# Second-layer block loads issued by SyncE, and another order of transposes, products, sets and FFN copies

## What is computed

```python
xn = layernorm(x)
h = relu(xn @ Wself0 + mean_of_neighbours(xn) @ Wneigh0 + b0)
gnn = h @ Wself1 + mean_of_neighbours(h) @ Wneigh1 + b1
q, k = relu(xn @ Wq + bq), relu(xn @ Wk + bk)        # 16 heads of 64
v = xn @ Wv + bv
mix = ((q @ k.T) / (1250 * 64) @ v) @ Wo + bo         # head by head
x = x + gnn + mix
y = layernorm(x)
out = x + quant(gelu(quant(y) @ ternary(w1).T)) @ ternary(w2).T
```

## Time and profile before

| | |
|---|---|
| median of 3 runs | 1304.35 us |
| the profiled execution | 1304.18 us |
| its span | 1302.4 us |
| TensorE busy | 1290.4 us, 99% |
| VectorE busy | 845.7 us, 65% |
| ScalarE busy | 652.0 us, 50% |
| GpSimd busy | 93.9 us, 7% |
| granted TensorE clock | 1.00 |

### The profile page before, as it was taken

One profiled execution on the slowest core, in us unless ns is written; L12 is line 12 of the kernel. 1 busy time (PEld: TensorE's weight loads), 2 busy tenths in 40 slices (PEclk: granted clock), 3 DMA queues, 4 the chain that ended last, 5 costly groups with the idle time before them and its releaser, 6 DMA issues.

```text
span 1302.4 us, 18781 instructions
## 1 busy us (share of the span) xinstructions
PE 1290.4 (99%) x6370; PEld 613.4 (47%) x6370; DVE 845.7 (65%) x1472; ACT 652.0 (50%) x895; POOL 93.9 (7%) x91
## 2 busy tenths in 40 slices
PE   9999999999999999999999999999999999999999
PEld 5454444555445444444444444444444444444444
DVE  6854542362677778975992663336787977786774
ACT  7766564364312246632442763547863376465460
POOL 0000000000000002100000110133440100000000
DMA  8498987764135466715877999999859939722523
GB/s 355 146 275 268 281 288 199 298 212 167 74 114 193 160 207 217 225 67 185 267 245 243 193 248 214 254 313 314 277 164 372 262 75 280 176 61 83 129 58 104
DMA packets 203093, 269.10 MB, mean 207 GB/s; under 512 B 110464, under 2 KB 144000, under 8 KB 199424
## 3 DMA queue, kind: packets, MB, share of 16 engines
q1 hardware_dynamic: 190432, 255.93, 62.8%
q10 hardware_dynamic: 11136, 6.82, 2.5%
q0 software_dynamic: 1440, 5.24, 2.2%
HBM read 184.33 MB, written 57.67 MB: 186 GB/s over the span
## 4 chain that ended last, share of the span: by engine, by line
PE 93%; DVE 3%; DMA 2%; issue 1%; ACT 1%; POOL 0%; ACTq 0%; SPq 0%; DVEq 0%
PE ps L2252 36%; PE ps L2533 13%; PE ps L2574 12%; PE ps L2684 9%; PE ps L2647 9%; PE ps L2383 8%; PE ps L2452 3%; PE ps L2391 1%; PE ps L2304 1%; DMA w1q_scratch<-STREAM 1%; PE ps L2286 1%; DMA SPLIT<-in_Wself 1%; DMA XIN<-in_x 0%; DVE Zb L1344 0%; PE ps L2729 0%
## 5 line engine op out<-in xcount | busy, mean ns | idle before, releaser
L2252 PE MATMUL ps<-S,XH 128*128 128x512 f16 x1440 | 317.1, 379 | 0.8 <-DVE Zb L1663 0.8
L2252 PEld LDWEIGHTS ps<-S,XH 128*128 128x128 f16 x1440 | 139.8, 98 | 165.7 <-DVE Zb L1663 2.7
L2252 PE MATMUL ps<-S,Zb 128*128 128x512 f16 x480 | 106.4, 379 | 0.0
L2383 PE MATMUL ps<-XH,S 128*128 128x512 f16 (+1 forms) x576 | 102.6, 340 | 0.0
L2252 PE MATMUL ps<-Zb,XH 128*128 128x512 f16 x432 | 94.8, 379 | 0.0
L1003 ACT ACTIVATE AT<-ps 128x320 f16<-128x320 f32 x40 | 17.4, 434 | 140.0 <-PE ps L2252 139.8
L2533 PE MATMUL ps<-XH,AT 128*128 128x512 f16 x400 | 86.8, 379 | 0.0
L2533 PE MATMUL ps<-Zb,AT 128*128 128x512 f16 x400 | 86.5, 379 | 0.0
L1616 DVE TENSOR_SCALAR STREAM<-tables,keys 128x320 f16 x240 | 71.1, 296 | 22.5 <-PE ps L2452 13.3
L2383 PEld LDWEIGHTS ps<-XH,S 128*128 128x128 f16 x576 | 56.0, 98 | 47.1 <-issue 2.3
L2252 PEld LDWEIGHTS ps<-S,Zb 128*128 128x128 f16 x480 | 46.9, 98 | 54.5 <-issue 0.6
(11 more groups left out here) (317 smaller groups left out, 1989.9 us busy)
## 6 DMA issues: line engine op xcount, KB each, us to landing
STREAM<-in_w_all SPq DMA_DIRECT2D x48, 512.0 KB, 5.1
STREAM<-in_w1t SPq DMA_DIRECT2D x42, 512.0 KB, 5.1
STREAM<-in_w2t SPq DMA_DIRECT2D x30, 512.0 KB, 5.1
XIN<-in_x SPq DMA_DIRECT2D x20, 512.0 KB, 5.1
Zb<-in_w1t SPq DMA_DIRECT2D x14, 512.0 KB, 7.2
blocks_scratch<-S SPq DMA_DIRECT2D x4, 1792.0 KB, 8.5
blocks_scratch<-STREAM SPq DMA_DIRECT2D x4, 1792.0 KB, 8.6
S<-blocks_scratch SPq DMA_DIRECT2D x7, 1024.0 KB, 14.4
```

Of the source, the lines that this page charges most:

```text
L2252: last = mm(acc[:, n * BANK:(n + 1) * BANK], left(l, kc), right(kc, r)[:, n * BANK:(n + 1) * BANK], start=(kc == 0 and i == 0), stop=(kc = ...
L2383: last = mm(ps[:, 3 * j * BANK + a:3 * j * BANK + b], Wq_s[:, kc, l, mc], XH[:, r, kc, a:b], start=(kc == 0 and l == 0 and r == 0), stop=( ...
```

## The change

Five places in the streams. (1) VectorE does `z0_lo(t)` ahead of `source_sum(4 + t)` in the first tiles. (2) The four loads of blocks into Zb leave ScalarE's stream and are issued by SyncE ahead of its transposes for the last pair; PE's order in items 0 and 1 and ScalarE's order of copies and square follow. (3) In items 5 to 9 `z1_lo_rest(i)` stands at the end of item i, ahead of `c11(i+1)`, and the third quad of an item after `c11` of the next one; the very last one after `z1_lo_rest(9)`. (4) In step G = 2 ScalarE has an order of its own (`f1_act_second`), two `hid_ints` stand earlier and `x2_ints(9)` later. (5) In step G = 4 the `sums` of pair 1 stand around step 3.

```diff
@@ -295,8 +295,12 @@
 
         def st_done(i, product):
 
+            if i == 0:
+                return dict(P1=1, P2=2, P6=3, P7=5, P5=6, P3=8, P4=9)[product]
             if product == "P1":
-                return 7 * i - 1 if i else 1
+                return 7 * i - 1 if i > 1 else 4
+            if i == 1 and product == "P2":
+                return 7
             if i == 2 * PAIRS - 1:
                 return 7 * i + dict(P2=2, P6=3, P5=4, P7=5, P3=6, P4=7)[product]
             return 7 * i + dict(P2=2, P6=3, P7=4, P5=5, P3=7, P4=8)[product]
@@ -587,6 +591,10 @@
                     if t + 2 < NT:
                         sp.wait_ge(S("h_t1"), t + 1)
                         s0_load(t + 2)
+                    if t == NT - 2:
+                        sp.wait_ge(S("g0_ps"), NT)
+                        for name in LOAD_ORDER[3:]:
+                            block_load(sp, 0, name)
                     if t == 2 * p:
                         h_turn_left(p)
                     elif p < PAIRS - 1:
@@ -1094,21 +1102,19 @@
 
                 for j in range(2):
                     t = 2 * p + j
-                    if t == NT - 1:
-                        act.wait_ge(S("g0_ps"), NT)
-                        for name in LOAD_ORDER[3:]:
-                            block_load(nc.scalar, 0, name)
                     act.wait_ge(S("h_t1"), t + 1)
                     A(TMP[:, j, :], TMP[:, j, :], ACT.Relu).then_inc(S("h_pos"), 1)
                     act.wait_ge(S("h_pos"), t + 1)
                     if j == 0:
                         wait(act, "h_turned0", 32 * p)
                         A(HL[:, 0, 0, :], TMP[:, 0, :], ACT.Copy).then_inc(S("h_hi"), 1)
+                    if t == NT - 1:
+                        act.wait_ge(S("c_x"), 1)
+                        st_copy(0, 0)
                     A(banks(4), TMP[:, j, :], ACT.Square, accum_out=at("h_sq", t)).then_inc(S("h_sq"), 1)
                 if p == PAIRS - 1:
-                    act.wait_ge(S("c_x"), 1)
-                    for which in range(3):
-                        st_copy(0, which)
+                    st_copy(0, 1)
+                    st_copy(0, 2)
                 wait(act, "h_turned1", 64 * p)
                 A(HL[:, 1, 0, BANK:D], TMP[:, 1, BANK:D], ACT.Copy).then_inc(S("h_hi"), 1)
                 act.wait_ge(S("h_sums"), 4 * p + 4)
...
@@ -1247,6 +1250,35 @@
                     alone(act)
                     gelu(t + 1, 0, 2 * g + s)
 
+            def f1_act_second():
+
+                G, p, t = 2, 1, 2
+                act.wait_ge(S("dq1"), t + 2)
+                for s in range(2):
+                    f1_copy(G, s, 1 + s, 0, 0, 8 * p - 4)
+                for s in range(2):
+                    f1_copy(G, s, 4 + 2 * s, 1, 0, 8 * p)
+                y_round(8)
+                y_std(9)
+                for s in range(2):
+                    f1_copy(G, s, 8 + 2 * s, 1, 1, 8 * p)
+                for s in range(2):
+                    act.wait_ge(S("f1_ps"), 14 * G + 11 + 2 * s)
+                    gelu(t, 1, s, F1_BANKS[s][0])
+                for s in range(2):
+                    act.wait_ge(S("f1_d"), 6 * G + 1 + s)
+                    alone(act)
+                    gelu(t, 0, s)
+                y_round(9)
+                for s in range(2):
+                    act.wait_ge(S("f1_d"), 6 * G + 3 + s)
+                    alone(act)
+                    gelu(t + 1, 1, s)
+                for s in range(2):
+                    act.wait_ge(S("f1_d"), 6 * G + 5 + s)
+                    alone(act)
+                    gelu(t + 1, 0, s)
+
             def hid_round(t, part=range(4)):
                 act.wait_ge(S("g_sc"), t + 1)
                 for n in part:
...
@@ -1779,9 +1811,8 @@
             for t in range(NT):
                 if t < KC:
                     prep_dve(t)
-                if t == 0:
-                    z0_lo(0)
                 if t < NT - 4:
+                    z0_lo(t)
                     source_sum(4 + t)
                 if t == NT - 4:
                     in_degrees()
...
@@ -1934,18 +1965,20 @@
 
                 quads = list(ST_QUADS[i])
                 c11(i)
-                if i > PAIRS:
-                    z1_lo_rest(i - 1)
+                for n in list(ST_QUADS[i - 1])[2:]:
+                    quad(n)
                 ahead = 0 if i == 2 else 1
                 for n in quads[:ahead]:
                     quad(n)
                 if i >= PAIRS:
                     z1_lo_first(i)
                 c22(i)
-                for n in quads[ahead:]:
+                for n in quads[ahead:2]:
                     quad(n)
                 c12(i)
                 c21(i)
+                if i >= PAIRS:
+                    z1_lo_rest(i)
 
             dve.wait_ge(S("h_sq"), NT)
             V.tensor_reduce(col("sq_h"), col("h_sq"), AXX, ALU.add).then_inc(S("added"), 1)
@@ -1966,7 +1999,8 @@
             times(col("deg_x"), col("deg"), col("tmp"))
             for i in range(1, 2 * PAIRS):
                 st_dve(i)
-            z1_lo_rest(2 * PAIRS - 1)
+            for n in list(ST_QUADS[2 * PAIRS - 1])[2:]:
+                quad(n)
 
 
             def x1_add(t):
...
@@ -2210,15 +2248,19 @@
             x1_rows(8)
             x2_block_sums(1)
             hid_ints(1, range(2))
-            x2_scaled(8, lambda: x1_add(9))
+            x2_scaled(8, lambda: (x1_add(9), hid_ints(1, range(2, 4))))
             x1_stats(9)
             x2_ints(8, 0)
-            hid_ints(1, range(2, 4))
-            f1_dve(1, 0, later(x2_scaled, 9), later(lambda: None), later(x2_ints, 9, 1))
-            f1_dve(1, 1, *(later(sums, 0, n) for n in range(2)), *(later(hid_max, 1, 0, 0, h) for h in range(2)))
+            f1_dve(1, 0, later(x2_scaled, 9))
+            f1_dve(1, 1, lambda: (x2_ints(9, 1), sums(0, 0)), later(sums, 0, 1),
+                   *(later(hid_max, 1, 0, 0, h) for h in range(2)))
             f2_dve(0, {(0, 0), (0, 1)})
             for p in range(1, NT // 2 - 1):
-                f1_dve(p + 1, 0, *(later(sums, p, n) for n in range(3)))
+                if p == 1:
+                    f1_dve(2, 0, later(lambda: None), later(lambda: None), *(later(sums, 1, n) for n in range(2)))
+                    sums(1, 2)
+                else:
+                    f1_dve(p + 1, 0, *(later(sums, p, n) for n in range(3)))
                 sums(p, 3)
                 f1_dve(p + 1, 1, *(later(hid_max, p + 1, 0, r, h) for r, h in ((0, 0), (0, 1), (1, 1), (1, 0))))
                 f2_dve(p, {(0, 0), (0, 1), (1, 1), (1, 0)})
@@ -2582,33 +2624,40 @@
 
             halves = (range(KC // 4), range(KC // 4, KC // 2))
 
-            def st_first(i, part=range(KC // 2)):
+            def st_first(i):
 
                 wait(pe, "st_c", 4 * (i - 2) + 3)
-                st_product(i, "P1", st_banks(i)[0], stop=False, part=part)
-
-            def st_pe(i):
-
-                a, b, c = st_banks(i)
+                st_product(i, "P1", st_banks(i)[0], stop=False)
+
+            def st_second(i):
+
                 wait(pe, "st_c", 4 * (i - 2) + 1)
                 if i == 1:
                     pe.wait_ge(S("h_sq"), NT)
-                st_product(i, "P2", b)
+                st_product(i, "P2", st_banks(i)[1])
+
+            def st_pe(i):
+
+                a, b, c = st_banks(i)
+                if i != 1:
+                    st_second(i)
                 pe.wait_ge(S("st_act"), 3 * i + 1)
                 st_product(i, "P6", a, False, False)
                 wait(pe, "st_c", 4 * (i - 2) + 4)
                 if i == 0:
                     pe.wait_ge(S("h_t1"), NT)
                 final = i + 1 == 2 * PAIRS
+                if i == 0:
+                    st_first(1)
                 st_product(i, "P7", c, stop=False, part=halves[0] if final else range(KC // 2))
-                if i == 0:
-                    st_first(i + 1, halves[0])
                 pe.wait_ge(S("st_act"), 3 * i + 2)
                 st_product(i, "P5", a, False, False)
                 if final:
                     st_product(i, "P7", c, False, False, halves[1])
+                elif i == 0:
+                    st_second(1)
                 else:
-                    st_first(i + 1, halves[1] if i == 0 else range(KC // 2))
+                    st_first(i + 1)
                 if i == 0:
                     h_total()
                 pe.wait_ge(S("st_act"), 3 * i + 3)
@@ -2658,7 +2707,7 @@
                 if G == 0:
                     pe.wait_ge(S("x1"), 7)
                 for s in range(2):
-                    wait(pe, "f1_act", 14 * (G - 1) + 10 + 2 * s)
+                    wait(pe, "f1_act", 14 * (G - 1) + (7 + s if G == 3 else 10 + 2 * s))
                     f1_product("P1", p, G, s, 0, stop=False)
                 if G == 2:
                     pe.wait_ge(S("x1"), NT)
@@ -2674,7 +2723,7 @@
                     pe.wait_ge(S("f1_act"), 14 * G + 3 + (1 if G == 2 else 2) * s)
                     f1_product("P5", p, G, s, 0, False, False)
```

(2 more changed lines are left out.)

17 lines of the change are left out of this document (9 added, 8 removed).

## The result

The changed kernel takes 1329.08 us, the median of 4 runs (1328.16 to 1330.1), against 1304.05 before in the same comparison: ratio 1.0193 with a 95% interval of 1.0178 to 1.0208, 25 us slower. The forecast was 1313.9, with a range up to 1318: the right side, less than half of the size. The profiled execution has a span of 1327.7 us against 1302.4.

The account below looks back on a forecast made before the run. TensorE computes 99% of the span, its waits total under 10 us, so reordering can win only those: 1304.2 - 0.7 - 1.5 + 9.8 + 3.6 - 1.5 = 1313.9 us, range 1303 to 1318.

Parts of the forecast that it names:

- A: First-layer tiles: low part first on VectorE removes PE's one wait of 0.77 us, less a little; -0.7.
- B: Second-layer item 0: block loads on SyncE and copies before ScalarE's square remove two PE waits; -1.5 us.
- the 790.8 of the sum: Item 0: time at which block T3 was forecast to land, ahead of PE wanting it at 793.1.
- The rival of late loads: Item 0: loads and transposes hinder each other in SyncE's queue, B +2 instead of -1.5; 1317 us, chance 0.07.
- C: Items 5 to 9 and x1 stage: third quad's store-load loop of 20.1 us exceeds PE's 18.14 an item; +9.8 us.
- I take 4.1: Items 5 to 9: assumed landing time in us of the HL load, within the loop's round trip of 20.1.
- D: FFN G=2 and G=3: copies ahead of y_round(8) delay it, new PE waits of 3.2 and 2.8; +3.6 us.
- E: FFN G=4: two quantisation sums moved behind the awaited VectorE sum remove PE's 1.5 us wait; -1.5.
- The other side: Whole kernel: all waits go and none comes, 1297.3 us, or 1303 with D as forecast; chance 0.13.
- the loop without contention: Items 5 to 9: POOL is not slowed by VectorE, so C is +2.3; 1306.4 us, chance 0.18.
- the FFN as meant: FFN G=2 and G=3: only D works as intended, -2.1, with C as forecast; 1308.2 us, chance 0.12.
- C's upper end: Items 5 to 9: about +14 us if the HL load takes 5.0.

Follow-up runs that it names:

- c_swap: Kernel before with part C alone, and SyncE issuing both loads ahead of both stores for third and next first quad: 1312.67 us against 1303.34, ratio 1.0055.
- c_alone: Kernel before with part C alone (z1_lo_rest at the item's end, third quad after the next item's c11): 1325.45 us against 1303.34, ratio 1.0162.
- d_alone: Kernel before with only D's edits (ScalarE's own order in G = 2, two hid_ints earlier, x2_ints(9) later): 1307.85 us against 1303.34, ratio 1.0041.
- abe: Kernel before with parts A, B and E together: 1301.5 us against 1303.34, ratio 0.9982.

## Why the prediction was right and wrong

- **A, -0.7: right.** The wait of the earlier trace rows is gone. Another has come later, since the low part of a later tile now waits for VectorE's own pace; the timeline after:

```profile
675.21 0.60 PE L2294 MATMUL ps<-S,XH 128*128 128x512 f16 x2 [0.44 <-DVE Zb L1695]
```

  What is left is 0.6 in this pair of traces. Over all traces, the stretch from PE's last L2452 product (L2494 after) to its first edge product takes 108.5 to 108.8 us in the ten without A, and 107.9 to 108.2 in the six with it.
- **B, -1.5: the mechanism is right, and the -1.8 of this pair is luck.** T3 landed earlier than the 790.8 of the sum. The DMA view and the timeline after have

```profile
Zb<-blocks_scratch SPq DMA_DIRECT2D x1, 1024.0 KB, 5.6
...
792.63 0.59 PE L2616 MATMUL ps<-Zb,XH 128*128 128x512 f16 x2
```

  and PE starts P7 at 792.63 without a wait. The transposes in the same queue were no hindrance: S<-SPLIT, issued just ahead of the loads, landed in 4.1 us, where in before one took 18.3 beside the loads of the other queue. The rival of late loads is refuted. The Trainium skill (DMA: Bandwidth & Descriptors, "Queues, rings and completion order") says that each DMA engine takes the descriptors of one queue in ring order; the 4.1 agrees. The step that was not looked at is how steady the old waits are: from item 0's first product to P6 of item 1 are 25.3 us in the trace of before, but 23.4 to 24.5 in eight other traces without B and 35.9 in c_swap's, and 23.4 to 23.5 in all six with B. So in eight of ten traces B would have won 1.1 us or less. The one of 35.9 was late block loads in the queue that B takes them out of.
- **C, +9.8: right mechanism, +22.0 measured** (19.0, 1.2 and 1.8; c_alone 22.1). This is the step that failed, and the term is the landing of the HL load, "I take 4.1": it was 8.0 from the first issue, 3.3 more than 0.6 + 4.1. With it the sum gives 23.4 us an item, against 23.0 and 24.0 seen; all other terms of the period held to 0.1. With the new order of SyncE's stream (c_swap) the same loads land in 4.5 and the three waits go. A second part: item 7 already waited 4.51, since the loop closes from item 6 on and the slack I had counted was one load's, which was longer too. A third: after the last wait, 5.26 us, the half clock took 1.9, and this is lost whole, while behind the earlier ones the loop, not PE, sets the next start. The first XIN load came 11.6 after the edge products' start (12.3 forecast), landed in 5.5, and the third tile waited 1.14 instead of 2.7:

```profile
995.66 1.72 SPq L636 DMA_DIRECT2D XIN<-u_scratch  x2
...
1001.28 1.28 DVE L2012 SCALAR_TENSOR_TENSOR TMP<-ps,cols,XIN 128x1024 f32<-128x1024 f32 x1 [8.61 <-DMA XIN<-u_scratch]
```

  The wait of 1.64 at G = 0 was in no term. ScalarE's first copies there wait for the store of a quad that stands in Zb, and SyncE, late through the whole x1 stage, issues it 0.3 us ahead of G = 0, where before it was 2.4 ahead:

```profile
1054.12 0.59 SPq L510 DMA_DIRECT2D w2q_scratch<-Zb  x1
...
1058.17 1.09 ACT L1222 ACTIVATE Zb<-ps 128x512 f32<-128x512 f32 x2 [1.02 <-DMA w2q_scratch<-Zb]
```

- **D, +3.6: right mechanism, +6.7 measured in G = 2 and 3.** The waits were 2.95 and 2.61 (forecast 3.2 and 2.8, which less the old 2.1 is 3.9 and not 3.6). ScalarE's operations that hold them up, from the timeline after:

```profile
1103.60 1.23 ACT L1199 ACTIVATE HL<-HL,cols 128x1024 f32<-128x1024 f32 x1
...
1115.60 1.23 ACT L1199 ACTIVATE HL<-HL,cols 128x1024 f32<-128x1024 f32 x1
...
1116.73 0.71 ACT L1214 ACTIVATE Zb<-Zb,cols 128x512 f32<-128x512 f32 x1
```

  y_round(8) starts 5.87 us after G = 2, as forecast (5.9). Missing was a term altogether, the clock: the five products behind the two waits take 3.2 us more. They have 4 matmuls each and start 0.86 apart otherwise. In the other direction, no term had that D takes the wait at G = 4 too, as d_alone shows. The timeline of PE:

```profile
1058.82 1.04 PE L2696 MATMUL ps<-S,tables 128*128 128x512 fp8e4 x4 [1.64 <-ACT Zb L1222]
...
1110.34 1.89 PE L2696 MATMUL ps<-STREAM,S 128*128 128x512 fp8e4 x4 [2.95 <-DVE Zb L2081]
...
1119.82 1.48 PE L2696 MATMUL ps<-S,tables 128*128 128x512 fp8e4 x4 [2.61 <-ACT Zb L1222]
```

- **E, -1.5: the time is right, its cause is shared.** The wait at G = 4 is gone, with E alone (abe) as forecast. But it is gone with D alone too, so in the full change the 1.5 can't be counted for E beside D.
- **The rivals.** The other side fell; the loop without contention fell by POOL's 2.01; the FFN as meant fell by the same waits. The range failed because C's upper end, +14, was bounded by a load of 5.0, when the trace of before had loads into HL of 12.1 in a saturated stretch, and because no case had a clock below 1.00: all of before's trace is at 1.00, and none of its waits is over 1.5 us.
